# Four sequence layers on one core: the slots of the layers' loop in another order

## The reference

```
h = x Win' + bin                                    # 2048 x 64
for each of 4 layers:
    y = silu(layernorm(h) * w + b)
    y = sconv(y)          # convolution with a damped complex rotation p^k, a recurrence over tokens
    h = h + y * scl
    y = layernorm(h) * w + b
    h = h + silu(y W1' + b1) W2' + b2               # 64 -> 256 -> 64 (two tiles of 128)
x = layernorm(x + layernorm(h) Wout' + bout)
Wg, Wu, Wd = codebook[idx_gate], codebook[idx_up], codebook[idx_down]    # 8192 rows of 8 values
x = layernorm(x + (silu(x Wg') * (x Wu')) Wd')      # 512 -> 1376 -> 512
```

## Time and profile before

| | us |
|---|---|
| three runs, median | 1266.31 (1262.34 to 1267.86) |
| the profiled execution | 1264.5 |
| its span, first to last instruction | 1262.5 |
| TensorE busy | 1188.8 (94%) |
| VectorE busy | 1011.6 (80%) |
| GpSimd busy | 929.9 (74%) |
| ScalarE busy | 261.7 (21%) |

### The profile page before, as it was taken

How to read it: one execution, slowest core, us unless ns; L and a number is a source line. 1 busy time by engine, 2 the same in 40 slices (tenths; PEclk the granted TensorE clock), 3 DMA queues, 4 the chain that set the end, 5 groups by cost and what they waited for, 6 DMA issues and landing times.

```text
span 1262.5 us, 16835 instructions
## 1 busy us (share of the span) xinstructions
PE 1188.8 (94%) x5595; PEld 839.3 (66%) x5595; DVE 1011.6 (80%) x2194; ACT 261.7 (21%) x395; POOL 929.9 (74%) x895
## 2 busy tenths in 40 slices
PE   6857998889999999999999999999999999999998
PEld 4533444346777777777777777777777777778876
DVE  3998898878997778888777888778888778888845
ACT  2325777772000000000000000000000000000024
POOL 6777777777777777777777777777777777777710
PEclk8968999989999999999999999999999999999999
DMA  9331211102433223433223433333433333334303
GB/s 202 64 68 37 45 37 39 27 4 53 105 92 87 65 71 80 95 82 92 65 69 79 89 85 81 65 70 86 93 85 87 67 70 79 94 72 88 60 2 133
DMA packets 96971, 93.57 MB, mean 74 GB/s; under 512 B 53549, under 2 KB 57909, under 8 KB 96886
## 3 DMA queue, kind: packets, MB, share of 16 engines
q1 hardware_dynamic: 64692, 83.86, 23.0%
q0 software_dynamic: 28160, 3.66, 8.5%
q10 hardware_dynamic: 4034, 4.98, 1.4%
HBM read 87.53 MB, written 4.90 MB: 73 GB/s over the span
## 4 chain that ended last, share of the span: by engine, by line
POOL 73%; issue 21%; PE 4%; DMA 1%; DVE 0%; ACT 0%; POOLq 0%; SPq 0%; DVEq 0%
POOL stage_down L400 57%; POOL stage_up L389 16%; PE bank L652 2%; PE cand L652 2%; DMA work<-in_L_ffn_idx_up 0%; DMA stage_down<-in_L_ffn_codebook,idx_down 0%; ACT x L505 0%; POOLq L160 0%; DVE chosen L1229 0%; DVE x L1033 0%; PE bank L924 0%; SPq L315 0%; DVE idx_low L1091 0%; DVE idx_low L1092 0%; DVE shift L1239 0%
## 5 line engine op out<-in xcount | busy, mean ns | idle before, releaser
L400 POOL DMA_INDIRECT stage_down<-in_L_ffn_codebook,idx_down x688 | 722.3, 1050 | 209.7 <-issue 209.1
L652 PE MATMUL cand<-one_hot,book 128*128 128x512 f32 (+1 forms) x2432 | 622.7, 398 | 19.0 <-DVE one_hot L1057 19.0
L1057 DVE TENSOR_SCALAR one_hot<-bc,low_of 128x512 fp32r<-128x512 uint16 (+1 forms) x1216 | 512.8, 482 | 99.0 <-PE cand L652 97.3
L652 PEld LDWEIGHTS cand<-one_hot,book 128*128 128x128 f32 x2432 | 449.7, 189 | 187.2 <-DVE one_hot L1057 51.8
L389 POOL DMA_INDIRECT stage_up<-in_L_ffn_codebook,idx_up x192 | 205.6, 1071 | 63.8 <-issue 58.2
L652 PE MATMUL bank<-x1t_hi,w 128*128 128x512 f32 (+1 forms) x704 | 239.1, 396 | 0.0
L1075 DVE SCALAR_TENSOR_TENSOR chosen<-bc,high_of,cand 128x512 f32<-128x512 uint16 (+1 forms) x304 | 220.2, 724 | 21.1 <-PE bank L652 17.9
L652 PEld LDWEIGHTS bank<-x1t_hi,w 128*128 128x128 f32 (+1 forms) x704 | 130.3, 185 | 31.4 <-issue 2.1
L652 PE MATMUL bank<-x1t_lo,w 128*128 128x512 f32 (+1 forms) x352 | 137.7, 391 | 0.0
L598 ACT ACTIVATE prod<-bank 128x512 f32<-128x512 f32 (+1 forms) x44 | 26.3, 599 | 389.4 <-PE bank L652 389.4
L605 ACT ACTIVATE act_hi<-prod 128x512 fp32r<-128x512 f32 x40 | 25.3, 633 | 342.5 <-DVE prod L1033 342.5
(11 more groups left out here) (181 smaller groups left out, 751.8 us busy)
## 6 DMA issues: line engine op xcount, KB each, us to landing
bc<-index_parts SPq DMA_DIRECT2D x272, 256.0 KB, 3.3
stage_down<-in_L_ffn_codebook,idx_down POOLq DMA_INDIRECT x688, 2.7
bc<-index_parts_rest SPq DMA_DIRECT2D x32, 192.0 KB, 3.1
x<-in_L_attn_x ACTq DMA_DIRECT2D x4, 1024.0 KB, 9.8
out_x<-x SPq DMA_DIRECT2D x16, 256.0 KB, 2.0
stage_up<-in_L_ffn_codebook,idx_up POOLq DMA_INDIRECT x192
index_parts<-parts_t SPq DMA_DIRECT2D x20, 32.0 KB, 2.0
w_in<-in_L_attn_W ACTq DMA_DIRECT2D x2, 256.0 KB
```

The lines of the kernel that those rows point to most:

```text
L400: pool.indirect_dma_start(stage_down[k % RING][:, q, j * CS:(j + 1) * CS], None, a["L0_ffn_codebook"], bass.IndirectOffsetOnAxis(ap=idx_do ...
L652: return pe.matmul(dst, lhs, rhs, start=start, stop=stop)
L1057: done = v.tensor_scalar(one_hot[quad % 2][:, q, 0:nw], bc[quad % BCS][:, 0:nw], low_of[:, q:q + 1], None, ALU.is_equal)
```

## The change

It touches the layers' loop alone. The same instructions are issued, in another order on three engines, with one more buffer.

- VectorE: `add_mixed(t-1)` moves from the slot's start to behind `choose` of the slot's first quad, so `one_hots` come first. `add_back` comes ahead of `norm2`. The damped result `d` has two buffers and waits for the mix of t-2, not t-1.
- TensorE: `mixed(t-1)` moves from ahead of the variances to behind `spread`. Its waits, and that of `back`, follow the new owners of `bank[0]`.
- ScalarE: `silus(t-2)` comes ahead of `square2(t-1)`.

```diff
-            work = at("work", [P, 13, C])
+            work = at("work", [P, 14, C])
...
-        sq1, rs1, xn, y, u, g, d = (work[:, n, :] for n in range(7))
+        sq1, rs1, xn, y, u, g = (work[:, n, :] for n in range(6))
+        d = [work[:, n, :] for n in (6, 13)]
...                                                  (ScalarE's slot)
+                if t >= 2:
+                    silus(t - 2)
                 if t:
                     square2(t - 1)
-                if t >= 2:
-                    silus(t - 2)
                 square1(t + 1)
...                                                  (TensorE)
             def mixed(i):
                 pe.wait_ge(s["damped"], i + 1)
-                if i >= 3:
-                    pe.wait_ge(s["h_made"], i - 2)
-                mm(bank[0][:, :], mix[:, i // NC, :], d).then_inc(s["mixed"], 1)
+                if i:
+                    pe.wait_ge(s["h_mid"], i)
+                if i >= 2:
+                    pe.wait_ge(s["h_made"], min(ITEMS - NC + 1, i - 1))
+                mm(bank[0][:, :], mix[:, i // NC, :], d[i % 2]).then_inc(s["mixed"], 1)
...
             def back(i):
                 pe.wait_ge(s["ff_made"], i + 1)
-                pe.wait_ge(s["h_mid"], min(ITEMS, i + 3))
+                pe.wait_ge(s["h_mid"], i + 2 if i < ITEMS - 3 else ITEMS)
...
-                if t:
-                    mixed(t - 1)
                 variance1(t)
...
                 if t >= 2:
                     spread(t - 2)
+                if t:
+                    mixed(t - 1)
                 for quad in quads[1:]:
                     candidates(quad)
...                                                  (VectorE's slot)
-                if t:
-                    add_mixed(t - 1)
                 one_hots(quads[0] + 1)
...
+                if t >= 3:
+                    add_back(t - 3)
                 if t >= 2:
                     norm2(t - 2)
-                if t >= 3:
-                    add_back(t - 3)
...
+                if t >= 2:
+                    v.wait_ge(s["mixed"], t - 1)
+                tt(d[t % 2], g, tab[:, l, :], ALU.mult).then_inc(s["damped"], 1)
+                choose(quads[0])
                 if t:
-                    v.wait_ge(s["mixed"], t)
-                tt(d, g, tab[:, l, :], ALU.mult).then_inc(s["damped"], 1)
-                choose(quads[0])
+                    add_mixed(t - 1)
                 for quad in quads[1:]:
```

## The result

| | before | after |
|---|---|---|
| median of 4 runs on the same chip, us | 1266.82 (1262.34 to 1267.86) | 1294.97 (1293.19 to 1295.56) |
| ratio | | 1.0227 [1.0200, 1.0253] |
| profiled execution, its span | 1264.5, 1262.5 | 1295.6, 1293.8 |
| mean granted clock | 0.982 | 0.966 |
| TensorE, VectorE, GpSimd, ScalarE busy | 1188.8, 1011.6, 929.9, 261.7 | 1209.2, 1014.0, 919.4, 263.3 |

The page of after: chain of work that ended last, and the granted clock in 40 slices.

A forecast was written before the change was run, and what follows sets the result against it. GpSimd's gathers and TensorE bound the kernel, ending level within 0.34 us. Loop +11.6, behind it +1.5, slow clock +1.0, less 0.34: +13.8 us on 1264.5, 1278.3 us profiled; 1279 forecast for the median, range 1271 to 1288.

The forecast's parts named there:

- GpSimd and TensorE level, so a gain is capped and a loss is whole: At the last tile's down weights both chains end within 0.34 us: gain at most 0.34, loop longer by X costs X - 0.34.
- The ring, 9.92 us: Layers' loop, add to next add through ScalarE's squares, table load, root and Silu, then VectorE: 9.92 us per plain slot.
- 13 steps in 133.0 us, loop +11.6: Loop from slot 2 to 15: 133.0 us against 120.4, 12.6 more; less 1.0 at the start, last add 11.6 late.
- the steps out of slots 4 and 8: Loop steps where the second quad's masks and choose follow the add: 10.05 us each, slot 4 with a keep_rest 10.7.
- the step out of slot 12: Loop step with two candidates and an add-up ahead of TensorE's variances, put 1.4 us late: 11.3 us.
- The two buffers hide the mix; Silus on ScalarE cost nothing: In the loop, the mix is there 0.9 us before the add wants it; Silus moved ahead end before square2 starts.
- The swap of `add_back` and `norm2` costs nothing while the clock is full: VectorE's slot: norm2 ends at A + 6.5, A the add's start, just in time for u at A + 6.6; cost nothing.
- Behind the loop +1.5: First variances behind the loop now stand behind the last add_mixed and both squares, at 2.0 us after the add: +1.5 us.
- Slow clock, "half a slot more of it than before, +1, with bounds of -2 and +10": In the loop a half-clock slot costs 2.3 us; half a slot more assumed, +1 us, bounds -2 (none) to +10 (four slots).
- the rival "the clock falls": TensorE's longer holes in the loop bring half clock back in half the slots: 15 us more, 1294 us; chance 0.08.
- The argument for it: For a falling clock: the loop's start, where it was sparse, ran at a granted clock of 0.83.
- the argument against it: Against a falling clock: holes of 1.4 us did no harm later; full clock from 125 to 245 us.

The follow-up runs named there:

- cap: Kernel before, leaving out one of three matmuls of each product in the first tile's hidden part (32 matmuls on TensorE): 1269.78 us, ratio 1.0015.
- the fill: Changed kernel plus up to two extra 128x512 matmuls per slot on TensorE ahead of the variances, results unread: 1282.49 us, ratio 1.0133 to the kernel before.
- `square1` first: Changed kernel with square1(t+1) ahead of square2(t-1) on ScalarE: 1284.78 us, ratio 1.0141 to the kernel before.
- Silus last: Changed kernel with square2(t-1) ahead of silus(t-2) on ScalarE again, as before the change: 1313.85 us, ratio 1.0348 to the kernel before.
- norm2first: Changed kernel with norm2(t-2) ahead of add_back(t-3) on VectorE again, as before the change: 1287.56 us, ratio 1.0180 to the kernel before.
- buffer: Kernel before with only the two buffers of d and the wait for the mix of the slot before the last: 1265.63 us, ratio 0.9982.

## Why the prediction was right and where it failed

- **GpSimd and TensorE level, so a gain is capped and a loss is whole.** Right. The last turn's wait is gone and the 32.0 us by which TensorE is late at the first turn arrive as 31.4 at the last and 31.3 in the span. `cap` shows the other side.
- **The ring, 9.92 us.** Right to 0.01 us in the plain steps at full clock, of which after has two and the fill eight. `square1` first (9.40) and Silus last (11.07) move it by the lengths of the steps they move.
- **13 steps in 133.0 us, loop +11.6.** Right where the clock is held: 134.0 with the fill. Its terms are less even: the steps out of slots 4 and 8 took 11.37 and 10.78 us there for 10.7 and 10.05, since VectorE waits for a late `back` in them (0.87 us out of slot 8), and the step out of slot 12 took 11.06 for 11.3. The adds of slot 2 stood at 115.5 forecast and 115.83 measured.
- **The two buffers hide the mix; Silus on ScalarE cost nothing.** Right: no wait of the add for TensorE in the plain slot, and `square2` starts 0.72 behind the add.
- **The swap of `add_back` and `norm2` costs nothing while the clock is full.** Right in plain steps, wrong by 0.39 us in the step out of slot 8 even at full clock; and the condition did not hold, at a price of 0.66 us in a slot at 0.84 or 0.85 (`norm2first`).
- **Behind the loop +1.5.** From the last add (263.15) to the first variances behind it:

```profile
263.15 0.68 DVE L1036 TENSOR_TENSOR h<-h,bank 128x512 f32<-128x512 f32 x1
...
265.06 1.20 PE L653 MATMUL bank<-work,mean_p 64*128 64x512 f32 x4
```

  1.91 instead of 0.54 is +1.4. But the first turn is 32.0 us late and the last add 263.15 - 236.94 = 26.2, so 5.8 us were lost behind the loop. The other 4.4 go with a clock of 0.83 there against 0.94 before. That the change caused them is not shown: in the profile of `buffer`, which has the order of before, the same way from the last `choose` to the first turn took 71.3 us against 67.9, with the clock at 0.84 from 245 to 300 us.
- **Slow clock, "half a slot more of it than before, +1, with bounds of -2 and +10".** This step failed. It measured 13.3 us in the loop, with 4.4 more behind it. The number of slots was wrong: seven of the 13 steps were below full clock. Their price was right in size (2.3 forecast; against the same steps of the fill 1.43 three times, 1.65, 2.13 and 2.53 twice, 1.9 on average). At the first turn the terms as measured are 11.6 + 1.3 (start and loop at full clock, against the forecast) + 13.3 + 1.4 + 4.4 = 32.0 us; 0.6 are given back by the last turn, and the profiled times differ by 31.1. The medians differ by 28.2: the profiled execution of before (1264.5) was one of its shorter ones.

So the rival "the clock falls", given 0.08, is what happened on top of the forecast ring. It put half of the 13 slots at half clock for 15 us (13.3 measured); that its 1294 fits the 1294.97 so closely is partly luck, since it counted nothing behind the loop. The argument for it read the 0.83 of the earlier trace rows as that of a sparse stretch; it is 94% busy, and TensorE's long waits (4.08 us up to 104.95, 1.90 us up to 115.28) lie ahead of it. What misled me was the argument against it: before, TensorE was idle for 13 of 120 us at full clock, in holes of 1.4 us. After, it is idle for 24 of 147: in the slots shown it stands 1.30 us ahead of the variances at 197.00, where the add-up fills part of the hole, and 0.40 and 2.08 us, one behind the other, ahead of those at 206.92. The prediction's own walk had this pause of 2.7 us where there had been 1.43, and I priced it by the holes of before instead of by the ones that the new order makes.

The length of the pause is not the whole cause, though. In after, TensorE stood 2.0 to 3.6 us ahead of the variances (in one step in part between them) in the seven steps that fell, and 0 to 1.3 us in five of the six that did not. But the sixth (variances at 242.01) had the same pauses of 0.40 and 1.85 us as the step at 152.52, which fell. And in `square1` first the way back at 170.98 took 3.44 us, half clock, behind pauses of only 0.83 and 0.43 us, shorter than the 1.43 that did no harm before.

The Trainium skill (TensorE: Matmul & The Clock Gate, HAM oscillation — how this bites in real kernels) describes a kernel whose bursts of matmuls have DMA waits of 3 to 5 us between them and fall back each time. The trace agrees in part: half-clock matmuls stand in a loop in which TensorE is busy 84% of the time, in seven of 13 steps and not in each, with pauses under 3 us but for one of 3.16, and the fill ends them in the loop.

What stays open: which slots fall. Steps of 9.92 and 12.45 stand side by side, and no run here shows what decides between them; the fill shows that TensorE's work in the loop sets the clock, not by what rule. Nor was a fill behind the loop tried, where the clock stayed low.

## What to carry to other kernels

Engines that work strictly down a list form rings: follow an instruction from engine to engine until it meets itself in the next turn, add start to start, and look for the second ring before you shorten the first; here they were 9.92 and 9.8 us, and taking the add out of one gained nothing on the other. When a reordering changes when TensorE pauses in each turn, price its matmuls at half clock in the steps that lie on the ring, even if pauses of that length did no harm in the old order, and test it with matmuls that nobody reads. And where two chains end level, as GpSimd's and TensorE's here, a shorter loop is worth nothing and a longer one costs its whole length.

## What the hardware showed unexpectedly

- A loop with TensorE 84% busy (123.23 of 147 us) ran at a mean clock of 0.90, one with 93% (133.36 of 143, the fill) at 0.99, one with 96% at 1.00; the loop of before had 1.00 with 89%. But `square1` first had 0.90 with 93% (125.84 of 135), as busy as the fill: the busy share does not sort the kernels by clock.
- GpSimd's row of the same 880 gathers took 927.9 us in one execution and 934.8 in another (before and `cap`); where it ends the kernel, as in both, the time follows. It is not all of the spread: of 19 executions of the kernel before on one chip, the six with a mean TensorE clock of 0.981 or more took 1263.3 to 1267.17 us and the seven with 0.976 or less 1268.67 to 1271.43.
- One chip ran the kernel before in 2173 us.
